# A graph network on one core: edge attributes in loads of 1024 edges, gathers and Relu counted in tiles of edges

## The chip, the cores and the metric

The kernel runs on one core of one Trainium2 chip. Time is the device time of one execution, in microseconds (us). An engine's name stands for its queue too: PE is TensorE, DVE VectorE, ACT ScalarE, POOL GpSimd, SP SyncE. PE multiplies, DVE and ACT work on elements, POOL here issues the indirect DMAs (gathers and scatters, whose addresses come from an index table), SP the plain ones.

## The reference

Four graph layers on 6250 nodes of 96 features and 206,250 directed edges, sorted by destination. The change touches the first two:

```python
h = jnp.maximum(_layernorm(x, axis=-1), 0.0)
# L0
m = h[src] + edge_attr_96                  # [206250, 96]
aggr = jax.ops.segment_sum(m, dst, num_segments=N_NODES)
x = x + (1.0 + eps[0]) * h + relu(aggr @ W1 + b1) @ W2 + b2
# L1
h = jnp.maximum(_layernorm(x, axis=-1), 0.0)
msg = jax.nn.relu(h[src] + edge_attr_32 @ We + be)
aggr = jax.ops.segment_sum(msg, dst, num_segments=N_NODES)
...
```

Behind them come a network of three convolution layers over the same edges and three attention layers with four heads.

## The kernel before

*Tiles, steps and groups.* Edges are cut into 1612 tiles of 128. Nodes are cut into 49 blocks of 128. Because edges are sorted by destination, a tile adds to one block, now and then to two or more; each pair of a tile and a block is a step, padded to 1664 steps. A step is one matmul: a one-hot matrix HOT (128 edges by 128 nodes of the block), built from `REL`, times the tile's 128 rows, into PSUM (`segment_group`, L854, matmul in L860). Eight steps (U) make a group; 208 groups. DVE adds each result to its block of `ACC`, whose number it reads into registers from the table `EB` (`add_up`, L1412, add in L1418). Which edge a step begins at is another row of `EB`, read by SP (`firsts`).

*HOT.* ACT builds it in `hot_of`, eight `Abs` operations (L647) and one `Relu` (L651) per group.

*L0.* A sum over edges of attributes, by `tile_sums` (PE), `load_tiles` (SP, L418) and `sum_stage` (DVE). `load_tiles` issues one DMA of 128 edges (48 KB, L427) per step into four slots of `G`, eight per group, behind the group that used the slot. The sum over neighbours `h[src]` goes another way: POOL scatters edges into a table of counts in DRAM (L582, 1625 indirect DMAs, in the same time as L0's first part), and the stage L0sum (the chase; PE in L885) multiplies strips of that table with the node features, split in bf16 parts by DVE (L1583 to L1585). Then come the layer's small matmuls (L0mlp), the normalisation and the store of the feature table in DRAM.

*L1.* Per group SP loads eight windows of 32 attributes (`load_attrs`, L402), PE transposes them (L966), ACT copies them back (`lift_attrs`, L670), PE multiplies them by We (L971), POOL gathers the rows `h[src]` of eight steps from the feature table (`sums_of`, L527, by `row_of`, L525), DVE adds the products to the gathered rows (`add_product`, L1604), ACT applies the Relu (L675), and PE and DVE sum as in L0. POOL takes the indices from `NOW`, into which DVE copies 16 at a time (L1432) behind the sums of two groups; this copy also tells POOL that the slots are free. All of it is counted in steps: a tile with two blocks is loaded, gathered and rectified twice.

The order on each engine is the order in which its function issues, with loops over four groups (`ROUNDS` = 52).

Of the kernel before, what the change touches and what calls it, by code (L numbers as in the profile page):

```python
# [5 lines left out]
def gnn_kernel(nc, x, src, dst, edge_attr_32, edge_attr_96, L0_W1, L0_b1, L0_W2, L0_b2, L0_eps,  # L6
# [17 lines left out]
    ds = bass.ds  # L24

    P = 128
    N, D = x.shape
# [28 lines left out]
    KC = -(-STEPS // P)  # L56
    WIDE = Q * P
# [16 lines left out]
    assert STRIPS % CHASE_RING == 0 and EP % ROWS_TOGETHER == 0 and 26 - LO_BITS + TALLY_BITS <= 24 and EF < 1 << TALLY_BITS  # L74
    assert SORTED < LOCAL and (PADS + 1) * P * LOCAL < 1 << 26 and SORTED <= 1 << 11

    ctx = ExitStack()
    with ctx:
# [16 lines left out]
        rel_rows = dram("rel_rows", [STEPS, P], bf16)  # L95

# [12 lines left out]
        HOT = sb("HOT", [P, 8, U, P])  # L109
        G = sb("G", [P, 8, U, WT])  # L110
        EA = sb("EA", [P, 2, U * D])
        NOW = sb("NOW", [P, 2, BT], i32)
# [29 lines left out]
        G_flat = G[:, :, :, :].rearrange("p s k d -> p (s k d)")  # L142
        HOT_flat = HOT[:, :, :, :].rearrange("p s k n -> p (s k n)")
# [38 lines left out]
        apart = [HOT[:, 2, :, :], H_flat[:, 0:U * P].rearrange("p (k n) -> p k n", k=U)]  # L182
        row_now = H_flat[:, U * P + TILES:U * P + TILES + 4 * U * P // 2].bitcast(bf16).rearrange("p (b a) -> p b a", b=4)
        assert U * P + TILES + 4 * U * P // 2 <= 3 * STEPS
        REL_neg = [HOT_flat[:, 3 * U * P:3 * U * P + TILES], H_flat[:, U * P:U * P + TILES]]
# [26 lines left out]
        def row(n):  # L212
# [12 lines left out]
        parts_ready = sem("parts_ready")  # L225
        iota_done, consts_done = sem("iota_done"), sem("consts_done")
# [25 lines left out]
        NAMES += [f"strip_in{n}" for n in range(RING)] + [f"tile_in{n}" for n in range(UN)]  # L252
# [8 lines left out]
        gather = {"idx_ready": GROUPS // 2}  # L261
        segment = {"apart_made": GROUPS, "hot_built": GROUPS, "seg_done": GROUPS, "acc_step": TILES}
        PARTED = PARTS + 1
        tiles = {f"tile_in{n}": ROUNDS * U * 16 for n in range(UN)}
# [7 lines left out]
        attrs = {"attr_in0": ITERS * U * 16, "attr_in1": ITERS * U * 16, "rows_ready": GROUPS}  # L272
        dense = {n: NG for n in ("prepared", "staged", "flipped", "lifted", "made", "taken")}
        MOVES = {
            "sum_attr": segment | tiles,
            "sum_relu": gather | segment | attrs | {"ea_flipped": GROUPS, "ea_lifted": GROUPS,
                                                    "ea_product": 2 * GROUPS, "summed": 2 * GROUPS},
# [38 lines left out]
        GATHERED = {name: [sem(f"gathered{slot}_{name}") for slot in range(UN if kind != "attend" else 8)]  # L316
# [14 lines left out]
        def firsts(k, n, engine):  # L331
            return nc.values_load_multi_w_load_instructions(
                EB[32:33, ds(k, n)], engines=(engine,), min_val=0, max_val=E - P,
                skip_runtime_bounds_check_because="the plan clips them")[1]
# [1611 lines left out]
```

## Time and profile before

| | us |
|---|---|
| median of 3 runs | 16749.57 (16744.98 to 16754.85) |
| profiled execution | 16653.95, its span 16652.1 |

| busy, share of the span | |
|---|---|
| PE | 6317.3 us (38%) |
| DVE | 5208.7 us (31%) |
| ACT | 4100.0 us (25%) |
| POOL | 8151.6 us (49%) |

No engine is busy for more than half the span: the kernel is a line of stages, each with its own limit, so shares of the whole say little. The slices of the page show the stages:

```profile
## 2 busy tenths in 40 slices
PE   0100005784444434799433333333333333333333
DVE  6200003422222222322433333343333334333334
POOL 2777771003555555100355555545555554555554
PEclk7555555586566666699655555555555555555555
GB/s 210 11 11 9 9 9 63 81 202 34 39 39 38 39 38 39 95 223 222 82 50 50 52 51 51 51 46 51 50 51 51 51 48 49 51 50 52 52 51 46
```

A slice is 416 us. Slices 2 to 6 are the scatter, in which PE and DVE do next to nothing; slices 7 and 8 are the rest of L0, slice 9 the chase, slices 10 to 16 L1, where POOL is at 5 tenths and PE at 4. From slice 20 on it is attention. In rows of matmuls below, one matmul of float32 counts as two records and two weight loads, so a group of eight steps is 16 records. "Remote" as the end of an idle time means that it was ended by an event that the profile can't put to an instruction close by. "Issue" means that the engine waited for nothing that the profile shows.

### The profile page before, as it was taken

Reading aid. Unit: us, or ns where it says so; the run is one execution under the profiler, and the core shown is the slowest. Engines: PE = TensorE matmul, PEld = TensorE weight load, DVE = VectorE, ACT = ScalarE, POOL = GpSimd, SP = SyncE. Lnnn points to the kernel's source line nnn. Section 1 sums busy time; section 2 is a strip of 40 time slices with the busy share of each in tenths; the row PEclk is TensorE's granted clock in tenths of the full one; section 3 lists DMA queues with packets and bytes.
Section 4 is the critical chain, followed back from the end, with each engine's and each line's share of the span. In section 5 each row is a group of like instructions: output and inputs, shape, how many; then the busy total and the mean of one; then the engine's idle time right before and its main releaser. Section 6 shows DMA issues by size and latency. Waiting matters only on the chain. (4 is left out here: it accounts for less than half of the span.)

```text
span 16652.1 us, 181011 instructions
## 1 busy us (share of the span) xinstructions
PE 6317.3 (38%) x36108; PEld 5357.2 (32%) x36109; DVE 5208.7 (31%) x16216; ACT 4100.0 (25%) x10462; POOL 8151.6 (49%) x8448
## 2 busy tenths in 40 slices
PE   0100005784444434799433333333333333333333
PEld 0000005762332322577432332323223233322332
DVE  6200003422222222322433333343333334333334
ACT  0000005702333333100222222222222222222222
POOL 2777771003555555100355555545555554555554
PEclk7555555586566666699655555555555555555555
DMA  6000002361221112377222222212222222222221
GB/s 210 11 11 9 9 9 63 81 202 34 39 39 38 39 38 39 95 223 222 82 50 50 52 51 51 51 46 51 50 51 51 51 48 49 51 50 52 52 51 46
DMA packets 1157570, 1039.16 MB, mean 62 GB/s; under 512 B 707670, under 2 KB 822582, under 8 KB 1157072
## 3 DMA queue, kind: packets, MB, share of 16 engines
q1 hardware_dynamic: 809536, 614.67, 13.3%
q0 software_dynamic: 265824, 340.03, 10.2%
q10 hardware_dynamic: 81744, 80.28, 1.5%
q14 instruction: 422, 3.46, 0.1%
q8 instruction: 44, 0.72, 0.0%
HBM read 940.04 MB, written 95.72 MB: 62 GB/s over the span
## 5 line engine op out<-in xcount | busy, mean ns | idle before, releaser
L525 POOL DMA_INDIRECT sb_G<-attention_table,sb_NOW x4992 | 4747.6, 951 | 3530.2 <-issue 1460.3
L860 PE MATMUL sums<-sb_G,sb_HOT 128*128 128x100 f32 (+2 forms) x16640 | 3443.1, 394 | 2724.0 <-ACT sb_HOT L651 1248.0
L860 PEld LDWEIGHTS sums<-sb_G,sb_HOT 128*128 128x128 f32 x16640 | 3285.0, 303 | 3012.0 <-issue 2756.1
L525 POOL DMA_INDIRECT sb_G<-feature_table,sb_NOW x1664 | 1573.9, 946 | 1330.8 <-DVE sb_NOW L1432 817.6
L1878 DVE TENSOR_TENSOR sb_ACC<-sb_ACC,sums 128x100 f32 x4992 | 1280.3, 256 | 2825.4 <-issue 1239.5
L582 POOL DMA_INDIRECT edge_counts<-sb_G x1625 | 1734.0, 1067 | 805.8 <-issue 535.3
L1418 DVE TENSOR_TENSOR sb_ACC<-sb_ACC,sums 128x97 f32 (+1 forms) x3328 | 849.9, 255 | 3956.5 <-remote 2447.7
L647 ACT ACTIVATE sb_H<-sb_iota_row,sb_H 128x128 f32<-128x128 f32 x4992 | 1528.7, 389 | 134.3 <-issue 45.5
L647 ACT ACTIVATE sb_HOT<-sb_iota_row,sb_HOT 128x128 f32<-128x128 f32 x3328 | 1015.4, 389 | 2008.8 <-remote 1381.1
L706 ACT ACTIVATE psC<-sb_SB 128x128 f32<-128x128 f32 x156 | 43.8, 281 | 5839.2 <-DVE sb_SB L1831 4863.5
L1037 PE MATMUL psD<-sb_lone,sb_HOT 1*128 1x4 f32 x312 | 90.7, 359 | 2213.3 <-DVE sb_lone L1838 1713.5
L1037 PEld LDWEIGHTS psD<-sb_lone,sb_HOT 1*128 1x128 f32 x312 | 77.2, 305 | 2228.0 <-DVE sb_lone L1838 1649.4
L971 PE MATMUL psB<-sb_WE,sb_EA 128*128 128x384 f32 x416 | 305.6, 833 | 1265.9 <-ACT sb_EA L670 1194.3
L1033 PE MATMUL psD<-sb_LW,sb_ones 128*128 128x128 f32 x312 | 124.1, 501 | 1726.8 <-DVE sb_LW L1796 1112.5
L564 POOL COPY sb_HOT<-sb_H 128x384 f32 (+1 forms) x104 | 54.3, 525 | 1456.4 <-DVE sb_H L1649 1072.3
L651 ACT ACTIVATE sb_HOT<-sb_H 128x1024 f32<-128x1024 f32 x624 | 659.8, 1057 | 66.8 <-remote 47.2
L1033 PEld LDWEIGHTS psD<-sb_LW,sb_ones 128*128 128x128 f32 x312 | 78.2, 311 | 1774.4 <-DVE sb_LW L1796 1143.9
L564 POOL COPY sb_HOT<-sb_ACC 128x384 f32 (+1 forms) x26 | 13.1, 508 | 1283.5 <-DVE sb_plan L1465 1202.4
L1750 DVE TENSOR_SCALAR sb_EA<-sb_H,sb_iota_col 128x1024 bf16<-128x1024 bf16 x624 | 293.8, 492 | 1087.9 <-remote 566.7
L1855 DVE TENSOR_TENSOR sb_G<-sb_G,psC 128x768 f32<-128x768 f32 x624 | 565.4, 948 | 3.6 <-issue 0.6
L670 ACT ACTIVATE sb_EA<-psA 128x256 f32<-128x256 f32 x208 | 79.9, 384 | 1921.3 <-remote 1490.4
L971 PEld LDWEIGHTS psB<-sb_WE,sb_EA 128*128 128x128 f32 x416 | 94.1, 282 | 1334.1 <-issue 1318.7
(435 smaller groups left out, 8993.4 us busy)
## 6 DMA issues: line engine op xcount, KB each, us to landing
sb_G<-edge_counts SPq DMA_DIRECT2D x1152, 256.0 KB, 3.3
sb_H<-rel_rows SPq DMA_DIRECT2D x624, 256.0 KB
sb_G<-in_edge_attr_dram SPq DMA_DIRECT2D x1664, 48.0 KB
sb_G<-attention_table,sb_NOW POOLq DMA_INDIRECT x4992
edge_counts<-sb_LW ACTq DMA_DIRECT2D x12, 6272.0 KB, 42.5
sb_EA<-in_edge_attr_dram SPq DMA_DIRECT2D x1664, 16.0 KB
sb_G<-feature_table,sb_NOW POOLq DMA_INDIRECT x1664
edge_counts<-sb_G POOLq DMA_INDIRECT x1625
```

Of the source, the lines that this page charges most:

```text
L525: pool.indirect_dma_start(to, None, rows, bass.IndirectOffsetOnAxis(ap=index, axis=0)).then_inc(landed, 16)
L582: pool.indirect_dma_start(every_count, bass.IndirectOffsetOnAxis(ap=slot_of[:, f:f + 1], axis=0), tally[:, f:f + 1], None).then_inc(scatte ...
L647: last = nc.scalar.activation(apart[place][:, c, :], iota_row[:, :], ACT.Abs, bias=REL_neg[place][:, ds(k + c, 1)])
L651: nc.scalar.activation(HOT[:, to, :, :], apart[place], ACT.Relu, bias=1.0, scale=-1.0)\
L860: last = nc.tensor.matmul(bank[:, k // 4, k % 4 * width:(k % 4 + 1) * width], HOT[:, hot, k, :], G[:, slot, k, 0:width], start=True, stop= ...
L971: nc.tensor.matmul((psB, psC)[q][:, 0:4 * D], EA[:, half, U * DE + q * P:U * DE + (q + 1) * P], WE[:, :, :].rearrange("p a b -> p (a b)"), ...
L1033: last = nc.tensor.matmul(psD[:, P:2 * P], ones[:, :], LW[:, 2, 0:P], start=True, stop=True)
L1037: last = nc.tensor.matmul(psD[:, 3 * P:3 * P + HEADS], HOT[0:1, BG * half, 0, :], lone[0:1, 4:8], start=True, stop=True)
L1418: v.tensor_tensor(to, to, sums[n % 2][:, k // 4, k % 4 * width:(k % 4 + 1) * width], ALU.add)\
L1750: v.tensor_scalar(ST[n % 2], row_now[:, n % 4, :].rearrange("p (k e) -> p k e", k=U), iota_col[:, 0:1], None, ALU.is_equal).then_inc(SEM[" ...
L1855: v.tensor_tensor(rows, rows, w.unsqueeze(3).broadcast_to([P, U, HEADS, C]), ALU.mult)\
L1878: v.tensor_tensor(to, to, sums[group % 2][:, k % U // 4, k % 4 * WT:(k % 4 + 1) * WT], ALU.add)\
```

## The change

*L0.* `load_tiles` loads 1024 edges (eight whole tiles, 384 KB) with one DMA into `ring0`, a ring of ten loads (80 tile places), 202 loads in place of 1664. Steps read the place of their tile in the ring from a new row of `EB`: PE loads eight places into registers per group (`places`, `sum_steps`), and each matmul addresses the ring by a register. A tile with two blocks is loaded once. Load g waits until g − 3 groups are summed, and group g waits for load g.

*L1.* One DMA per 1024 edges of attributes, 202 groups of products; POOL gathers tile by tile (1612 gathers) into `ring1` of twelve groups, waits ahead of gathers g until g − 5 groups are summed (`seg_done`), and for indices once per 48; add_product and Relu run once per tile, 202 groups; PE's sums address `ring1` by registers too. HOT's differences are built in another buffer (place=1).

*Indices by tile.* Ahead of the chase ACT loads the sources tile by tile, DVE casts them, PE transposes them in 13 pieces, DVE copies them out, and ACT stores them (`src_cols`) and loads them again as `cols_now` beside the chase. Two rows of places are computed on DVE in the setup.

```diff
+    LOADS = -(-ET // U)
+    LAST_LOAD = ET - (LOADS - 1) * U
+    LAG = -(-(NB - 1) // U)
+    RING0, RING1, SIX = 10, 12, 6
...
+        def places(ring, k, n, engine):
+
+            row, top = (32, RING0 * U - 1) if ring is ring0 else (0, RING1 * U - 1)
             return nc.values_load_multi_w_load_instructions(
-                EB[32:33, ds(k, n)], engines=(engine,), min_val=0, max_val=E - P,
+                EB[row:row + 1, ds(k, n)], engines=(engine,), min_val=0, max_val=top,
...
+            def load_attrs(t, attr):
+
+                to = [EA[:, half, 0:U * DE].rearrange("p (k d) -> p k d", k=U) for half in range(2)]
+
+                def load(g, half):
+                    sp.dma_start(to[half], tiles_of(attr, U * g, U)).then_inc(SEM[f"attr_in{half}"], 16)
...
             def load_tiles(t, attr):
 
-                with sp.Fori(0, ROUNDS) as it:
-                    for half in range(2):
-                        e = firsts(UN * U * it + 2 * U * half, 2 * U, SP)
-                        for j in range(2 * half, 2 * half + 2):
-
-                            sp.wait_ge(SEM["seg_done"], UN * it + (freed(t, UN) + j + 1))
-                            for n in range(U):
-                                sp.dma_start(G[:, j, n, 0:D], attr[ds(e[j % 2 * U + n], P), :])\
-                                  .then_inc(SEM[f"tile_in{j}"], 16)
+                def emptied(g):
+
+                    sp.wait_ge(SEM["seg_done"], g + (t.base["seg_done"] + LAG + 1 - RING0))
+
+                def load(g, slot):
+                    emptied(g)
+                    sp.dma_start(ring0[:, U * slot:U * (slot + 1), 0:D], tiles_of(attr, U * g, U)).then_inc(attr_in[slot], 16)
...
             sp.wait_ge(rel_rows_made, 1)
             sp.dma_start(rel_rows.rearrange("(c p) e -> p c e", p=P), rel_row).then_inc(rel_rows_stored, 16)
+            sp.wait_ge(rel_rows_stored, 16)
...
             def sums_of(t):
 
-                with pool.Fori(0, ROUNDS) as it:
-                    for pair in range(UN // 2):
-
-
-                        pool.wait_ge(SEM["idx_ready"], UN // 2 * it + (t.base["idx_ready"] + pair + 1))
-                        pool.sem_inc(idx_seen, 1)
-                        for n in range(2 * U):
-                            slot = 2 * pair + n // U
-                            row_of(G[:, slot, n % U, 0:D], NOW[:, pair, n:n + 1], table, t.gathered[slot])
+                def rows(g, six, slot, tiles):
+
+                    pool.wait_ge(SEM["seg_done"], g + (t.base["seg_done"] + LAG + 1 - RING1))
+                    if slot % SIX == 0:
+
+                        pool.wait_ge(SEM["idx_ready"], six + (t.base["idx_ready"] + 1))
+                    pool.sem_inc(idx_seen, 1)
+                    for n in range(tiles):
+                        at = slot % SIX * U + n
+                        row_of(ring1[:, U * slot + n, :], NOW[:, slot // SIX, at:at + 1], table, t.gathered[slot % SIX])
...
+            act.wait_ge(rows_in, 5 * 16)
+            act.wait_ge(parts_ready, 1)
+            full = ET // P * P
+            act.dma_start(src_tiles[:, 0:full].rearrange("p (c e) -> p c e", e=P),
+                          src_rows[0:full, :].rearrange("(c t) e -> t c e", t=P)).then_inc(tiles_loaded, 16)
...
+            act.wait_ge(cols_made, 1)
+            act.dma_start(src_cols, src_turned[:, 0:SIXES * SIX * U]).then_inc(cols_stored, 16)
...
+            act.dma_start(cols_now, src_cols).then_inc(cols_in, 16)
...
-                nc.scalar.activation(G[:, half, :, 0:D], G[:, half, :, 0:D], ACT.Relu).then_inc(SEM["rows_ready"], 1)
+                rows = ring1[:, ds(U * slot, U), :]
+                nc.scalar.activation(rows, rows, ACT.Relu).then_inc(SEM["rows_ready"], 1)
...
+            def sum_steps(t, g, half, ring, width):
+
+                place = places(ring, U * g, U, PE)
+                pe.wait_ge(SEM["acc_step"], U * g + (t.base["acc_step"] - U))
+                pe.wait_ge(SEM["hot_built"], g + (t.base["hot_built"] + 1))
+                for k in range(U):
+                    last = nc.tensor.matmul(sums[half][:, k // 4, k % 4 * width:(k % 4 + 1) * width], HOT[:, half, k, :],
+                                            ring[:, ds(place[k], 1), 0:width].squeeze(1), start=True, stop=True)
+                last.then_inc(SEM["seg_done"], 1)
...
-            pe.wait_ge(parts_ready, 1)
+            pe.wait_ge(tiles_cast, 1)
+            for c in range(KC):
+                last = nc.tensor.transpose(sums[c // 8][:, c // 4 % 2, c % 4 * P:(c % 4 + 1) * P],
+                                           src_turning[:, c * P:(c + 1) * P], ident[:, :])
+            last.then_inc(tiles_turned, 1)
+            pe.wait_ge(cols_made, 1)
             chase_stage(Stage("L0sum"))
...
+            def turn(g, half, nth, products=True, rows=True):
+
+                if products:
+                    attr_product(half + 1, 16 * nth + t.base[f"attr_in{1 - half}"], g + 2, g + 1)
+                if rows:
+                    pe.wait_ge(SEM["rows_ready"], g + (t.base["rows_ready"] + 1))
+                sum_steps(t, g, half, ring1, D)
...
+            dve.wait_ge(tiles_loaded, 32)
+            v.tensor_copy(src_turning, src_tiles).then_inc(tiles_cast, 1)
+            dve.wait_ge(tiles_turned, 1)
...
+            last.then_inc(cols_made, 1)
             dve.wait_ge(zeroed, 16 * NG)
             chase_sums(Stage("L0sum"))
```

On SP, in L0's loop, stood this before; `sb_G` is the ring of four slots, L332 the register load of the edges at which steps begin:

```order
L332 TENSOR_LOAD sb_EB
L425 ISA
L427 ISA [waits seg_done]
L427 DMA sb_G<-in_edge_attr_dram 128x96
L427 ISA
L427 DMA sb_G<-in_edge_attr_dram 128x96
```

and now this, for two groups (`sb_HG` holds `ring0`):

```order
L465 ISA
L462 ISA [waits seg_done]
L462 DMA sb_HG<-in_edge_attr_dram 128x8x96
L458 REGISTER_ALU
L462 ISA [waits seg_done]
L462 DMA sb_HG<-in_edge_attr_dram 128x8x96
L458 REGISTER_ALU
```

The register loads are gone from SP, and eight pairs of a register step and a DMA have become one.

On PE, one group of L0 was this before:

```order
L868 ISA [waits hot_built]
L858 ISA [waits tile_in0]
L860 MATMUL sums<-sb_G,sb_HOT 128x97 [waits acc_step]
L860 MATMUL sums<-sb_G,sb_HOT 128x97 x7
L867 REGISTER_ALU
```

and is now this (the two last rows stand eight times in all):

```order
L354 ISA [waits attr_in_ring0]
L354 TENSOR_LOAD sb_EB
L934 REGISTER_ALU
L935 REGISTER_ALU [waits acc_step]
L937 ISA [waits hot_built]
L937 MATMUL sums<-sb_HG 128x97
L937 ISA
L937 MATMUL sums<-sb_HG 128x97
```

The load of places has come to PE, ahead of the waits for DVE's adds and for HOT, and a register operation has come between any two matmuls. In L1 the same rows stand behind the wait for `rows_ready`.

On POOL, L1's gathers stood like this before, 16 behind one wait for indices:

```order
L529 ISA
L525 DMA sb_G<-feature_table,sb_NOW 128x96 [waits idx_ready]
L525 DMA sb_G<-feature_table,sb_NOW 128x96 x15
L533 REGISTER_ALU
L525 DMA sb_G<-feature_table,sb_NOW 128x96 [waits idx_ready]
```

and stand like this now:

```order
L579 ISA [waits seg_done]
L570 DMA sb_HG<-feature_table,sb_NOW 128x96 [waits idx_ready]
L570 DMA sb_HG<-feature_table,sb_NOW 128x96 x7
L576 REGISTER_ALU
L570 DMA sb_HG<-feature_table,sb_NOW 128x96 [waits seg_done]
L570 DMA sb_HG<-feature_table,sb_NOW 128x96 x7
```

A wait for a summed group has come ahead of every eight gathers, and the wait for indices stands at every sixth of them.

## Rows read from the trace of the kernel before

**Rows 1.** Windows: busy us of each engine (records), granted clock, DMA share, GB/s.

```profile
647.00:2560.00 1913.00, 167.60 (x720) 156.94 (x720) 92.83 (x345) 157.45 (x405) 1451.23 (x1383) 0.50 0.06 10
2600.00:3380.00 780.00, 587.82 (x2560) 550.22 (x2560) 331.18 (x1288) 564.17 (x1449) 0.00 (x0) 0.51 0.35 80
...
3440.00:3770.00 330.00, 311.38 (x2558) 238.26 (x2556) 40.24 (x93) 0.28 (x1) 1.02 (x3) 0.99 0.76 237
...
3880.00:6740.00 2860.00, 1225.32 (x4596) 833.25 (x4597) 650.88 (x2187) 939.44 (x2291) 1575.87 (x1668) 0.62 0.20 38
```

**Rows 2.** Timeline of DVE beside the scatter: start us, us, operation, idle before it.

```profile
1556.40 3.06 DVE L1418 TENSOR_TENSOR sb_ACC<-sb_ACC,sums 128x97 f32 x8 [41.89 <-remote]
```

**Rows 3.** SP's line L427, 700 to 2560 us: min/median/max ns; who waited.

```profile
L427 SPq DMA_DIRECT2D sb_G<-in_edge_attr_dram x351: 8/699/1400, 701.1 to 2560.0; - x176
...
  PE sums L860: 199.0, 6
```

**Rows 4.** The same line, 2700 to 3300 us.

```profile
L427 SPq DMA_DIRECT2D sb_G<-in_edge_attr_dram x986: 332/333/333, 2699.8 to 3300.0; - x198
```

**Rows 5.** Timeline of SP beside the scatter.

```profile
1517.60 24.53 SPq L427 DMA_DIRECT2D sb_G<-in_edge_attr_dram  x7
```

**Rows 6.** PE's line L860, 2600 to 3400 us: idle before it, us and times.

```profile
  DVE sb_ACC L1418: 330.8, 244
  DMA sb_G<-in_edge_attr_dram: 88.7, 66
```

**Rows 7.** Timeline of DVE after the scatter.

```profile
2912.49 3.06 DVE L1418 TENSOR_TENSOR sb_ACC<-sb_ACC,sums 128x97 f32 x8 [1.32 <-PE sums L860]
2917.98 3.06 DVE L1418 TENSOR_TENSOR sb_ACC<-sb_ACC,sums 128x97 f32 x8 [2.43 <-PE sums L860]
2921.99 3.06 DVE L1418 TENSOR_TENSOR sb_ACC<-sb_ACC,sums 128x97 f32 x8 [0.95 <-PE sums L860]
```

**Rows 8.** Groups by line, 3880 to 6740 us: busy us, mean ns, idle before.

```profile
L525 POOL DMA_INDIRECT sb_G<-feature_table,sb_NOW x1664 | 1573.9, 946 | 1330.8 <-DVE sb_NOW L1432 817.6 <-issue 513.2
```

**Rows 9.** Timelines of POOL and DVE in L1.

```profile
4915.81 0.95 POOL L525 DMA_INDIRECT sb_G<-feature_table,sb_NOW  x1 [0.30 <-issue]
4923.87 0.95 POOL L525 DMA_INDIRECT sb_G<-feature_table,sb_NOW  x1 [7.11 <-DVE sb_NOW L1432]
...
4919.71 3.03 DVE L1418 TENSOR_TENSOR sb_ACC<-sb_ACC,sums 128x96 f32 x8 [10.23 <-remote]
...
4928.32 3.03 DVE L1418 TENSOR_TENSOR sb_ACC<-sb_ACC,sums 128x96 f32 x8 [4.29 <-PE sums L860]
```

**Rows 10.** Timeline of DVE in the setup.

```profile
480.18 1.03 DVE L1318 CAST sb_H<-sb_H 128x1664 f32<-128x1664 int32 x1 [138.72 <-DMA sb_H<-dst_rows,sb_row_i]
```

**Rows 11.** Line L337, register loads and steps on PE's queue (PEldq), ns.

```profile
L337 PEldq TENSOR_LOAD <-sb_EB x624: 587/591/775, 8095.8 to 16593.6; - x156
L337 PEldq FUSED_REGOPS  x600: 46/46/51, 8198.7 to 16551.5; - x150
```

**Rows 12.** Timeline at the end of L0.

```profile
3389.63 3.06 DVE L1418 TENSOR_TENSOR sb_ACC<-sb_ACC,sums 128x97 f32 x8 [1.18 <-PE sums L860]
...
3430.63 1.62 PE L885 MATMUL sums<-sb_HOT,sb_G 128*128 128x288 bf16 x6 [41.14 <-DVE sb_HOT L1585]
```

**Rows 13.** DMAs by what they move: KB each, median us to landing.

```profile
feature_table<-sb_ACC SPq DMA_DIRECT2D x1, 2496.0 KB, 10.9
```

**Rows 14.** Groups by line, whole span: PE, then DVE.

```profile
L783 PE MATMUL sums<-sb_ident,sb_H 128*128 128x128 f32 x13 | 5.3, 412 | 141.6 <-DVE sb_G L1319 141.6
...
L1329 DVE CAST sb_IDX<-sums 128x512 int32<-128x512 f32 (+1 forms) x4 | 2.4, 592 | 0.1
```

**Rows 15.** Timeline of POOL in attention.

```profile
9020.20 0.95 POOL L525 DMA_INDIRECT sb_G<-attention_table,sb_NOW  x1 [3.79 <-remote]
...
9054.19 0.95 POOL L525 DMA_INDIRECT sb_G<-attention_table,sb_NOW  x1 [13.43 <-PE sums L860]
```

**Rows 16.** Line L525 from 8100 us on: min/median/max ns, first, last start.

```profile
L525 POOL DMA_INDIRECT sb_G<-attention_table,sb_NOW x4992: 942/947/1209, 8106.0 to 16565.8; - x200
```

## What I predicted before the run

> **What bounds the kernel now.** I read the windows by stage first, then for each stage that the change touches its groups by line, its waits, and the timeline of a few groups. The profiled execution took 16653.95 us (span 16652.1).
>
> The windows [rows 1] show the four stretches that the change touches. From 647 to 2560 us POOL is busy for 1451 of 1913 us with the scatter (L582) while PE does 720 matmul records beside it. One group of eight steps is 16 records, so that is 45 of 208 groups. From 2600 to 3380 POOL is silent and PE does 2560 records, 160 groups in 780 us: 4.87 us each. From 3440 to 3770 the chase keeps PE busy for 311 of 330 us. From 3880 to 6740 L1 runs, with POOL the busiest engine at 1576 of 2860 us. What follows 6740 keeps its instructions.
>
> *L0 beside the scatter.* DVE adds up one group in 3.06 us and idles for 41.9 us before it [rows 2]: a group takes 44.9 us here and 4.87 us later, with the same work. The adds are not slower themselves (3.06 us in both, rows 2 and 7). What is slow are SP's queue steps: the issue of a DMA has a median of 699 ns here and 333 ns after the scatter [rows 3, 4]. Seven issues take 24.53 us [rows 5], 4.0 us from one to the next with three instructions each (register operation, move, issue), so about 1.3 us per instruction, near twice 0.7. I read this as one path, taken up while POOL issues DMAs back to back, that lets one instruction through per 0.7 us and that SP and PE use in turn. The count bears it out: per group SP has 8 times 3 and about 2 more for the register loads, PE 32 records and about 4 register and wait steps, 62 to 64 together; 64 times 0.7 is 44.8 us.
>
> *L0 after the scatter.* PE's sums wait 330.8 us on DVE's adds and 88.7 us on attributes [rows 6]. DVE's groups of 3.06 us start 5.49 and 4.01 us apart [rows 7]. The shorter is what the chain of PE and DVE does when the tile is there; SP's eight issues, with their register loads, make the rest.
>
> *L1.* POOL's 1664 gathers of 946 ns leave it idle for 1330.8 us, 817.6 of them on DVE's copy of indices (L1432) and 513.2 between issues [rows 8]: 1252 ns per gather while it issues. Around 4900 us [rows 9] a burst of 16 ends at 4916.76 and POOL then waits 7.11 us until DVE has copied the next 16 indices: 19.7 and 7.1 us, 27 for two groups, 13.5 to 13.7 each. DVE's adds idle 10.23 us there "until remote", and are released 2.95 us after POOL's last gather: the same slow spell. The next group, out of the spell, is added up 8.61 us later. So L1 is a loop: a burst of gathers, a spell in which the news that a group is summed comes late, and a restart that waits for that news.
>
> **The change part by part.** Durations are of the profiled execution; the median of the runs shown (16749.57) is 96 us longer, and I carry a difference in us over to it unscaled.
>
> *Rows of places.* Twelve more DVE operations of 1664 elements on one row, at 1.03 us or up to twice that: 12 to 25 us. They stand ahead of the 138.72 us in which DVE waits for dst_rows [rows 10]. Cost 0; without this cover up to 25.
>
> *L0 beside the scatter.* SP goes from about 26 instructions per group to 4. PE gains per group a register load, three register and wait steps and a register operation for each matmul: 12 beside 32 records, 44. By the count above 48 times 0.7 is 33.6 us, and I take 34. About 1900 us of scatter then hold 56 groups instead of 45. Bounds: if PE alone sets the pace (44.9 over 36 is 1.25 each), 44 times 1.25 is 54.8 us and some 37 groups; on the other side the case in which the spell goes altogether, a rival below.
>
> *L0 after the scatter.* 152 groups instead of some 162. A load of 1024 edges is one issue, made once the group four before is summed: 13 us ahead, against 10.9 us for a transfer six times its size in rows 13. So SP no longer decides. PE's register load is 591 ns and a register step 46 ns [rows 11]. They stand ahead of the wait for DVE's adds and run while the matmuls of the group before are still queued, so PE needs 3.7 to 4.7 us. I take 4.25 us, between the 4.01 of rows 7 and 4.7; bounds 3.9 and 4.87. 152 times 4.25 is 646 us: L0 ends near 2576 + 646 = 3222 instead of 3392.7, where its last adds end [rows 12], 170 us earlier. With 54.8 and 4.87 it would be 171 groups in 833 us, an end near 3409 and a loss of 17; with 34 and 3.9 the gain is 224. A group in 4.25 us asks for 0.39 MB, 92 GB/s; this stretch moves 80 now and the chase 237 [rows 1], so the transfers are not the bound.
>
> The Trainium skill (DMA: Bandwidth & Descriptors, Rules for kernel authors) says to coalesce many small transfers, since under 64 KB one pays mostly overhead. By it the 48 KB tiles are the fault in both stretches. The trace agrees after the scatter, where SP's steps fill the gap; beside the scatter PE waits 199.0 us of 1913 for attributes [rows 3], so size is not what holds it there. By that rule alone L0 would end with the scatter, which I do not follow.
>
> *In front of the chase.* PE starts the chase at 3430.63, behind DVE's last cast [rows 12]. Between them come now a load of the sources as tiles (806 KB; 2496 KB take 10.9 us, a third of it 3.6 [rows 13]), a cast like the one of 1.03 us in rows 10, 13 transposes of 5.3 us and four copies of 2.4 us in all [rows 14]. That is 12 to 20 us, and with the handovers between four queues I take 20; bounds 10 and 40. The store and the load of 0.84 MB run beside the chase, 7 us at 237 GB/s if nothing hides them; PE is the bound there, so 0.
>
> *L1.* 202 groups instead of 208, 1612 gathers instead of 1664. POOL asks that the group six before is summed and issues eight gathers, instead of 16 per copy of indices. The ring holds twelve groups. A burst of eight takes 8 times 1.252 less the last pause, 9.7 us. What follows it is the question. Attention runs POOL so already, eight gathers per group summed [rows 15]: a gap of 3.79 us ahead of 9020.20, next to none within the 16 gathers that follow, then 13.43 us. Its 4992 gathers lie between 8106.0 and 16565.8 [rows 16], 13.6 us per group with all that lies between its layers, and its groups are more work. I take 3.15 us, near the 2.95 from the last gather to the release in rows 9: 12.9 us per group. 202 times 12.9 is 2606, and the last six groups without gathers and the start some 65: 2671. Now it is 208 times 13.7, 2851. Gain 180. Bounds: POOL without any gap, 10.05 us per group, a gain of 755; a gap of 7.1 us behind every eight (as now behind every sixteen), 16.8 us, a loss of 610. Of the gaps the 3.79 of rows 15 stands in the same setting, so I stay near it.
>
> *Sum.* −170 + 20 − 180 = −330: 16654 becomes 16324, and 16750 becomes 16420.
>
> **The rivals.**
>
> *A. POOL runs through in L1.* For it: a group out of the spell takes 8.61 us, less than POOL's 10.05, and the ring of twelve lets POOL be five groups ahead. Against it: beside the scatter a group in a lasting spell takes 44.9 us, so PE falls behind until the ring is full and POOL must wait; attention with its ring of eight does that. At 10.05 to 11.5 us (10.8): 202 × 10.8 + 65 = 2247, a gain of 604, with the other terms 754: 15996.
>
> *B. SP's own eight DMAs per group make the spells.* For it: SP's steps are what the profile shows slow in L0. Then L0 ends inside the scatter, the chase begins near 2600 instead of 3430 (830 less), and L1 is POOL's 10.05 (755 less): 15165. Against it: POOL in attention waits 13.43 us for PE's sums [rows 15] with a single load per group on SP. Beside it stands a sentence of the Trainium skill (DMA: Bandwidth & Descriptors, SWDGE vs HWDGE vs iDMA): DMAs issued by SP never touch the ring state that GpSimd writes. Taken widely it would leave SP's issues alone while POOL issues; rows 3 and 4 show 699 ns against 333, and the measurement decides.
>
> *C. Slower: L1's restarts feed the spell.* POOL restarts at each sum, so a new spell begins about as PE starts the next one, and PE is later by its register load and steps, which stand behind the wait for the rows (591 + 12 × 46, 1.1 us). If this pushes the news of each group behind the end of the burst, POOL waits 7.1 us or more behind each eight. It decides from a gap of 4.1 us on (2851 less 65 is 2786, over 202 is 13.8, less 9.7). At 7.1 us L1 takes 3459, a loss of 608, and with L0's 150 less the total is 17208. For it: the 13.43 in rows 15. Against it: the 3.79 there and the 16 gathers almost without a gap, and that five groups lie between POOL and PE instead of two to four.
>
> *D. Nothing to measure.* L0 at 54.8 us per group beside the scatter and L1 at 13.8.
>
> **How the numbers follow.** The forecast, 16420, has 0.60, with a range of its own of 16250 to 16620. A has 0.16, B 0.04, C 0.14, D 0.06. About 0.2% (33 us) is what a measurement of this kernel can tell from no change. Faster by more: the forecast, A, B and a little of D, 0.81; within it 0.06; slower 0.13. The range from 15880 to 16860 leaves out B, the low edge of A and most of C.
>
> **What would show it.** Right: DVE's adds beside the scatter 32 to 36 us apart; after it PE's groups 4.1 to 4.4 us apart; PE's first chase matmul 15 to 30 us behind the last cast; POOL in bursts of eight with gaps of 2.5 to 4 us in L1. Wrong: adds beside the scatter still 45 us apart or more (PE's records alone set the spell) or 4 to 9 us (B), POOL without gaps (A), gaps over 5 us behind each burst (C), or PE waiting for attributes behind the big load.

## The result, and the profile after

The changed kernel took 16241.22 us (median of 4 runs, 16235.82 to 16251.36), the kernel before 16750.93 in the same comparison: ratio 0.9697, 95% interval 0.968 to 0.9714. That is 510 us less; 330 were forecast. In the profiled executions the difference is 418 us (16652.1 and 16233.8 us of span), since the one of before was 97 us under its median. A second pair on one chip (c1 and c2 below) gave 16602.74 and 16113.32 us, ratio 0.9703; in its two traces the difference is 473 us.

Windows of the changed kernel, columns as in rows 1:

```profile
647.00:2560.00 1913.00, 162.72 (x704) 152.61 (x704) 97.24 (x344) 155.28 (x401) 1451.39 (x1373) 0.50 0.06 10
...
3000.00:3100.00 100.00, 90.67 (x392) 84.98 (x391) 50.08 (x195) 85.34 (x222) 0.00 (x0) 0.50 0.38 97
```

Beside the scatter nothing has moved: 704 records, 44 groups, against 45 [rows 1]. After it 392 records in 100 us are 24.5 groups, 4.08 us each against 4.87; over all 164 groups of this stretch it is 4.11 us against 4.82. The timelines of PE and DVE beside the scatter, then of SP's line L462 (min/median/max ns):

```profile
1028.65 3.72 PE L937 MATMUL sums<-sb_HG 128*128 x16 [41.36 <-issue]
...
1024.91 3.06 DVE L1512 TENSOR_TENSOR sb_ACC<-sb_ACC,sums 128x97 f32 x8 [42.02 <-remote]
1069.99 3.06 DVE L1512 TENSOR_TENSOR sb_ACC<-sb_ACC,sums 128x97 f32 x8 [42.02 <-remote]
```

```profile
L462 SPq DMA_DIRECT2D sb_HG<-in_edge_attr_dram x42: 367/373/377, 709.3 to 2558.7; - x42
```

PE's matmuls end at 1032.37 and DVE adds their results from 1069.99 on, 37.6 us later; for most of that time only POOL works. A group takes 45.1 us, as before (44.9, rows 2). SP now issues once per group, at the moment when the news comes, and in 373 ns.

At the end of L0 and in front of the chase:

```profile
3292.06 3.06 DVE L1512 TENSOR_TENSOR sb_ACC<-sb_ACC,sums 128x97 f32 x8 [0.98 <-DVE sb_ACC L1512]
...
3338.14 1.03 DVE L1653 CAST sb_H<-sb_H 128x1664 f32<-128x1664 int32 x1 [5.34 <-DMA sb_H<-src_rows]
3339.28 2.63 PEld L1036 LDWEIGHTS sums<-sb_ident,sb_H 128*128 128x128 f32 x13 [48.62 <-issue]
3339.32 3.01 PE L1036 MATMUL sums<-sb_ident,sb_H 128*128 128x128 f32 x13 [48.41 <-DVE sb_H L1653]
3342.36 2.08 DVE L1657 CAST sb_H<-sums 128x512 int32<-128x512 f32 x4 [3.19 <-PE sums L1036]
...
3344.78 7.93 PE L966 MATMUL sums<-sb_HG 128*128 128x288 bf16 x48 [2.46 <-DVE sb_H L1657]
```

L0's last adds end at 3295.1 instead of 3392.7 [rows 12], 98 us earlier, although the scatter's last DMA starts at 2593.1 and not at 2576.0. Between the end of the last cast (3332.8) and the first matmul of the chase lie 12.0 us instead of 0.4.

L1 by lines (columns as in rows 8), and POOL and DVE in a piece of it:

```profile
L570 POOL DMA_INDIRECT sb_HG<-feature_table,sb_NOW x1612 | 1524.6, 946 | 966.8 <-issue 463.4 <-remote 405.9 <-DVE sb_NOW L1685 65.4
```

```profile
4807.85 0.95 POOL L570 DMA_INDIRECT sb_HG<-feature_table,sb_NOW  x1 [4.42 <-remote]
...
4832.85 0.95 POOL L570 DMA_INDIRECT sb_HG<-feature_table,sb_NOW  x1 [4.13 <-remote]
...
4856.77 0.95 POOL L570 DMA_INDIRECT sb_HG<-feature_table,sb_NOW  x1 [4.21 <-remote]
...
4807.11 3.03 DVE L1512 TENSOR_TENSOR sb_ACC<-sb_ACC,sums 128x96 f32 x8 [0.50 <-remote]
...
4832.11 3.03 DVE L1512 TENSOR_TENSOR sb_ACC<-sb_ACC,sums 128x96 f32 x8 [3.98 <-remote]
```

Bursts of sixteen gathers now start 24 to 25 us apart here, instead of 27 [rows 9]. Counted over all of L1, the trace has 100 gaps of more than 1.9 us between gathers, 84 of the 99 distances between them are sixteen gathers, and the median gap is 3.5 us; before it was 100 gaps, 97 distances of sixteen, and 7.3 us. So the bursts have kept their length, although POOL now asks ahead of every eight, and the gap has become shorter. The first gather starts at 3799.2 and the last at 6224.3: 2425 us, 12.0 per group of 202, against 2838 (3881.2 to 6719.6). POOL starts 0.74 us after DVE has the news (4807.85 and 4807.11), where it used to start 4.16 us after (4923.87 and 4919.71, rows 9): DVE's adds and copy no longer stand in between.

The difference of 413 us splits by rows 8 and the row above: 49 us busy and 50 us between issues, both with 52 gathers fewer, and 314 us of waiting (817.6 less 65.4 at the start, against 405.9 and 32.2 on sums). Part of it comes back at the end. Behind the start of the last gather DVE adds up twelve more groups, six of which have no gathers of their own:

```profile
6229.43 3.03 DVE L1512 TENSOR_TENSOR sb_ACC<-sb_ACC,sums 128x96 f32 x8 [5.40 <-PE sums L937]
...
6280.36 3.03 DVE L1512 TENSOR_TENSOR sb_ACC<-sb_ACC,sums 128x96 f32 x8 [0.79 <-DVE sb_ACC L1512]
6284.18 3.03 DVE L1512 TENSOR_TENSOR sb_ACC<-sb_ACC,sums 128x96 f32 x8 [0.79 <-PE sums L937]
```

The first six are 8.9 to 9.8 us apart and the last ones 3.82, up to 6302.6: 78 us from the last gather on, where it was 11.

### The profile page after: what moved, and what is told of

It is laid out like the page before. It is cut to its first block, busy times and chain, and to the rows that moved or that the text cites. A ratio compares the mean times of both kernels' runs of the same rounds, so it can differ in the third digit from the quotient of the medians.

```text
span 16233.8 us, 175253 instructions
## 1 busy us (share of the span) xinstructions
PE 6413.5 (40%) x36085; PEld 5433.4 (33%) x36086; DVE 5208.3 (32%) x16151; ACT 4094.3 (25%) x10450; POOL 8110.2 (50%) x8396
## 4 chain that ended last, share of the span: by engine, by line
another core or an unknown queue 26%; issue 25%; DVE 17%; PE 16%; DVEq 11%; ACT 4%; DMA 1%; ACTq 1%; SPq 0%; POOL 0%; POOLq 0%; PEldq 0%
PE sums L927 5%; DVE sb_ACC L1973 4%; PE sums L995 3%; DVEq L1973 3%; DVE sb_ACC L1512 3%; ACT sb_H L699 2%; DVEq L1971 2%; DVEq L362 2%; DVE sb_EA L1845 1%; ACT sb_HG L739 1%; PE sums L966 1%; DVE sb_HG L1950 1%; DVEq L1830 1%; PE sums L937 1%
## 5 line engine op out<-in xcount | busy, mean ns | idle before, releaser
L570 POOL DMA_INDIRECT sb_HG<-attention_table,sb_NOW x4992 | 4741.1, 950 | 3566.9 <-issue 1454.7
L937 PE MATMUL sums<-sb_HG 128*128 x6656 | 1446.8, 405 | 2418.1 <-issue 2243.7
L937 PEld LDWEIGHTS sums<-sb_HG 128*128 128x128 f32 x6656 | 1351.0, 310 | 2691.1 <-issue 2691.1
L927 PE MATMUL sums<-sb_HG 128*128 128x100 f32 x9984 | 2065.4, 398 | 364.5 <-DVE sb_HG L1950 345.7
L634 POOL DMA_INDIRECT edge_counts<-sb_HG x1625 | 1748.2, 1076 | 808.7 <-issue 539.2
L927 PEld LDWEIGHTS sums<-sb_HG 128*128 128x128 f32 x9984 | 1998.3, 308 | 393.7 <-issue 378.1
L699 ACT ACTIVATE sb_H<-sb_iota_row,sb_H 128x128 f32<-128x128 f32 x6656 | 2037.1, 388 | 151.7 <-issue 54.3
L570 POOL DMA_INDIRECT sb_HG<-feature_table,sb_NOW x1612 | 1524.6, 946 | 966.8 <-issue 463.4
L699 ACT ACTIVATE sb_EA<-sb_iota_row,sb_HG 128x128 f32<-128x128 f32 x1664 | 508.6, 387 | 1905.7 <-remote 1764.4
L703 ACT ACTIVATE sb_HG<-sb_H 128x1024 f32<-128x1024 f32 x832 | 879.2, 1057 | 75.0 <-issue 25.1
L1950 DVE TENSOR_TENSOR sb_HG<-sb_HG,psC 128x768 f32<-128x768 f32 x624 | 565.1, 947 | 0.0
```

Source lines behind the costliest of these rows:

```text
L570: pool.indirect_dma_start(to, None, rows, bass.IndirectOffsetOnAxis(ap=index, axis=0)).then_inc(landed, 16)
L634: pool.indirect_dma_start(every_count, bass.IndirectOffsetOnAxis(ap=slot_of[:, f:f + 1], axis=0), tally[:, f:f + 1], None).then_inc(scatte ...
L699: last = nc.scalar.activation(apart[place][:, c, :], iota_row[:, :], ACT.Abs, bias=REL_neg[place][:, ds(k + c, 1)])
L703: nc.scalar.activation(HOT[:, to, :, :], apart[place], ACT.Relu, bias=1.0, scale=-1.0)\
L927: last = nc.tensor.matmul(bank[:, k // 4, k % 4 * width:(k % 4 + 1) * width], HOT[:, hot, k, :], G[:, slot, k, 0:width], start=True, stop= ...
L937: last = nc.tensor.matmul(sums[half][:, k // 4, k % 4 * width:(k % 4 + 1) * width], HOT[:, half, k, :], ring[:, ds(place[k], 1), 0:width]. ...
```

## The experiments

The runs came to several chips, and these fell into two kinds, which nobody chose. On one kind (the comparison above, and c1 to c4 on chip 11) the kernel before takes 16587 to 16755 us; on the other (e on chip 10, d and f on chip 14) its medians are 12618 to 12637. Each experiment is read within its kind. No chip was seen in both kinds, but chip 14 alone was used twice, so it is not shown that the kind belongs to the chip and not to the time of the run.

### e1: eight DMAs per group again

```diff
-                    sp.dma_start(ring0[:, U * slot:U * (slot + 1), 0:D], tiles_of(attr, U * g, U)).then_inc(attr_in[slot], 16)
+                    for n in range(U):
+                        sp.dma_start(ring0[:, U * slot + n, 0:D], attr[ds(P * U * g + P * n, P), :]).then_inc(attr_in[slot], 16)
```

> The changed kernel, but L0 loads each 1024 edges in eight DMAs of 128 edges again (same ring, same waits). Compared with the changed kernel. Theory of the prediction (SP and PE share one path, 0.7 us per instruction): SP's instructions per group rise from 4 to about 20, a group beside the scatter takes 64 x 0.7 = 45 us and more, clearly longer than in the changed kernel if that count were what matters there. Rival (SP's instructions cost nothing beside the scatter, since the wait there is for PE's news alone): adds stay 45.1 us apart there, and only the stretch after the scatter changes, from 4.3 to about 4.6 to 4.9 us per group for some 163 groups: L0 ends 50 to 95 us later, the total is longer by as much.

(PE's waits count the eight DMAs of a load accordingly.) 12587.92 us against 12617.65 of before, ratio 0.9977 (0.9967 to 0.9987). There was no late news to test, and L0 is over at 1515 us, inside the scatter, so nothing that it costs can show in the total. It says nothing on either theory of the lateness. Its trace does say what the transfers themselves cost where the news is on time: groups are 4.33 us apart against 4.12 in e3 on the same chip, which loads 1024 edges at once, and L0 ends 48 us later (1515 against 1467). The expectation had 4.6 to 4.9.

### e2 and f1: every matmul of L0's sums twice

```diff
-                for k in range(U):
+                for k in [k for k in range(U) for _ in range(2 if ring is ring0 else 1)]:
```

> The changed kernel, but every matmul of L0's sums is issued twice (64 instead of 32 records and weight loads per group; the second overwrites the first). Rival A (beside the scatter PE's news comes only after each of its matmul and weight records has passed, about 1.3 us each): adds are 82 to 87 us apart beside the scatter, some 24 groups done by its end. Rival B (the news is late by a fixed 37 us, whatever PE did): 49 us apart. The theory of the prediction (0.7 us per instruction, 76 of PE and 4 of SP): 56 us. After the scatter PE alone sets 7.5 to 8 us per group in all cases, so the total grows by about 600 (B) to 750 us (A).

> As e2: every matmul of L0's sums issued twice. On a chip on which PE's news is late: 82 to 87 us between adds beside the scatter if the news waits for each of PE's matmul and weight records (A), 49 us if it is late by a fixed time (B), 56 us by the prediction's count of instructions. On a chip without late news nothing is learned.

12596.12 and 12599.29 us (one run each; before 12617.65 and 12636.71). L0 lies beside the scatter here, so the total could not show it; but the groups did not become slower either. They are 4.11 us apart, as in e3 (4.12), where PE alone was expected to need 7.5 to 8. Windows of e2, then of e3:

```profile
700.00:1400.00 700.00, 647.94 (x5445) 620.77 (x5446) 349.86 (x1361) 596.23 (x1533) 530.75 (x556) 1.00 0.41 96
...
700.00:1400.00 700.00, 619.24 (x2724) 579.44 (x2723) 349.82 (x1362) 595.41 (x1531) 531.07 (x555) 0.52 0.40 96
```

With 32 matmul records per group the granted clock was 1.00 (2.4 GHz), with 16 it was 0.52, almost all of it the lower level of 1.2 GHz. So the 32 records of a group took 3.81 us, where 16 take 3.72: twice the work in the same time. What the lateness depends on could not be learned, since both runs came to chips without it.

### e3, d2 and f2: L1 asks once per two groups; e4: asks three groups nearer

```diff
-                    pool.wait_ge(SEM["seg_done"], g + (t.base["seg_done"] + LAG + 1 - RING1))
+                    if slot % 2 == 0:
+                        pool.wait_ge(SEM["seg_done"], g + (t.base["seg_done"] + LAG + 2 - RING1))
```

and in e4 `LAG + 4` in the first of these lines.

> The changed kernel, but in L1 POOL asks for summed groups only ahead of every second group and for both at once, so that it issues 16 gathers in a burst as before the change; ring, tiles and everything else stay. If L1's gain comes from bursts of eight (finer asking), L1 goes back to about 13.5 us per group, from 12.0: 300 us longer. If it comes from being released by the sum itself rather than by DVE's copy, or from the deeper ring, L1 stays near 12.0 to 12.5 and the total within 100 us.

> The changed kernel, but in L1 POOL waits until g - 2 groups are summed before it gathers for group g, instead of g - 5: bursts of eight stay, the depth that the ring allows is not used. If depth is what gains, POOL waits longer for each group and L1 goes to 14 us per group and more (400 us longer). If POOL is always at the limit of the wait anyway (it restarts at the news of each group whatever the distance), only the start differs, and the total stays within 50 us.

> As e3: in L1 POOL asks once per two groups and for both at once, 16 gathers in a burst. On a chip on which PE's news is late: if bursts of eight are what gained in L1, 13.5 us per group and 300 us more than the changed kernel's 2387 us of gathers; if the release by the sum itself and the depth of five groups are, near 12 us and no more than 100 us. On a chip without late news: no difference, 2011 us.

> As d2: in L1 POOL issues 16 gathers per asking. On a chip on which PE's news is late: L1's gathers last 2387 us in the changed kernel (11.9 per group); some 2700 if bursts of eight are what gained, below 2490 if the release by the sum and the depth of five groups are.

e3 12587.59 (0.9976, 0.9967 to 0.9986), e4 12588.14 (0.9975), d2 12599.68 (0.9981, 0.9972 to 0.9991), f2 12614.94 us against 12636.71 (one run each). All came to the second kind of chip. POOL's line there, in e3 (from 2600 to 4700 us, with its idle time):

```profile
L570 POOL DMA_INDIRECT sb_HG<-feature_table,sb_NOW x1612: 940/944/1000, 2611.8 to 4622.9; - x180
...
  issue: 491.0, 1611
  DVE sb_NOW L1686: 65.4, 1
```

POOL never waits for a sum: 2011 us for 1612 gathers, 9.96 per group. So how and how far ahead it asks makes no difference there, and which of burst, depth and direct release gained L1's time on the first kind of chip was not measured by a run. The trace of the changed kernel narrows it: its bursts were still sixteen gathers long, so bursts of eight are not what gained.

The same kernel beside the scatter, timelines of DVE and POOL:

```profile
1002.77 3.06 DVE L1513 TENSOR_TENSOR sb_ACC<-sb_ACC,sums 128x97 f32 x8 [0.98 <-DVE sb_ACC L1513]
1007.10 3.06 DVE L1513 TENSOR_TENSOR sb_ACC<-sb_ACC,sums 128x97 f32 x8 [1.27 <-issue]
...
1002.80 0.96 POOL L635 DMA_INDIRECT edge_counts<-sb_HG  x1 [0.30 <-issue]
1004.07 0.95 POOL L635 DMA_INDIRECT edge_counts<-sb_HG  x1 [0.30 <-issue]
```

The groups are 4.04 and 4.33 us apart and not 45. Adds last as long as on the other chips (3.06 us), and so does the median scatter (0.96 us). POOL's stream is not quite the same, though. On the first kind its scatters become longer around each release of the news:

```profile
1070.13 1.12 POOL L634 DMA_INDIRECT edge_counts<-sb_HG  x1 [0.30 <-issue]
1072.14 1.91 POOL L634 DMA_INDIRECT edge_counts<-sb_HG  x1 [0.89 <-issue]
```

From the first scatter to the last it takes 2319 us in the changed kernel there (274.0 to 2593.1) and 2158 in e3 (274.5 to 2432.4). So most of the difference between the kinds is the news that comes late or on time, and 140 to 160 us of it are POOL's own slower stream.

### c1 and c2: both kernels, unchanged

> The kernel before, unchanged, for a trace of it on the chip of the experiments, where its time was 12618 us and not 16750. If the late news from PE (adds beside the scatter 44.9 us apart, L1 at 13.7 us per group) is what is missing there, L0 is over before the scatter ends, L1's gathers go without gaps (1664 x 1.25 = 2080 us), and attention's 4992 gathers too (2090 us per layer instead of 2740). If instead the whole chip is faster, single gathers and adds are shorter as well (946 and 257 ns here).

> The changed kernel, unchanged, on the chip of the experiments. Where PE's news is not late, L0 costs nothing beside the scatter, and what is left of the change is 52 gathers fewer (65 us) less the work in front of the chase (12 us): some 50 us, 0.4%, faster than before, 12565 to 12590. Where the news is late, 16240 against 16750 again.

c1 16591.81 us, c2 16113.32 (5 runs) against 16602.74, 0.9703 (0.969 to 0.9717). This chip is of the first kind. c1 repeats the trace before: 720 records from 647 to 2560 us, L1's gathers over 2838 us, attention's over 2721 to 2738 us a layer. On the other kind (e3) attention takes 2089 to 2095 us a layer. The second case of each expectation, a chip without late news, could not be seen for these two kernels. The variants e1, e3, e4 and d2 come near it: their traces show L0 inside the scatter or POOL never waiting in L1, and their gain over before is 0.19 to 0.25%, 20 to 30 us. That the unaltered change gains as much there is an inference and was not run.

### c3 and c4: the scatter waits for L0

```diff
+    START_GATE, GATE, GATE_GROUPS = 240, 6, 1
...
+                        issued += 1
+                        if issued >= START_GATE and (issued - START_GATE) % GATE == 0 and asked + GATE_GROUPS <= GROUPS:
+                            asked += GATE_GROUPS
+                            pool.wait_ge(SEM["seg_done"], Stage("L0").base["seg_done"] + asked)
```

In c4 `GATE_GROUPS` is 2.

> The changed kernel, but POOL's scatter pauses: after every six of its DMAs it waits for one more group of L0 to be summed. Where PE's news is late while POOL issues without a pause: a group every 11 to 12 us beside the scatter instead of 45, all 208 groups by about 3000 us, L0 ends some 250 us earlier. Where the news is not late: the scatter is held up by nothing (a group takes less than six DMAs' 7.6 us), no difference.

> The same, but two more groups asked for after every six DMAs. Late news: the first group comes 3 us after POOL stops and the second 4 to 9 us later, so a turn takes 16 us for two groups: L0 done by about 2350 us and the scatter by 3100 (or earlier if both come together). Not late: two groups at about 4.3 us each need 8.6 us against the six DMAs' 7.6, so the scatter is held up by 1 us per turn, some 100 us in all.

c3 took 15455.53 us and c4 15517.74 (one run each) on the chip where the changed kernel takes 16113.32. For c3 that is 658 us less, 4.1%, and 6.9% less than before. The window of c3 beside the scatter, and POOL, DVE and PE in it:

```profile
647.00:2560.00 1913.00, 791.02 (x3441) 733.22 (x3441) 480.50 (x1687) 728.76 (x1874) 1281.32 (x1317) 0.51 0.19 44
```

```profile
1011.94 0.96 POOL L636 DMA_INDIRECT edge_counts<-sb_HG  x1 [0.30 <-issue]
1015.43 0.96 POOL L636 DMA_INDIRECT edge_counts<-sb_HG  x1 [2.53 <-remote]
...
1032.66 0.96 POOL L636 DMA_INDIRECT edge_counts<-sb_HG  x1 [2.39 <-remote]
...
1015.29 3.06 DVE L1518 TENSOR_TENSOR sb_ACC<-sb_ACC,sums 128x97 f32 x8 [9.78 <-remote]
...
1001.68 3.72 PE L943 MATMUL sums<-sb_HG 128*128 x16 [7.38 <-DVE sb_ACC L1518]
1006.20 3.72 PE L943 MATMUL sums<-sb_HG 128*128 x16 [0.80 <-issue]
```

PE's matmuls of two groups end at 1005.4 and 1009.9. POOL stops at 1012.9, and at 1015.29, 2.4 us after, DVE, PE and POOL all go on. That repeats every 17.2 us (12 DMAs, two groups). Adding POOL's pauses is the only edit, and with them the news comes 9.9 us after the first group's matmuls (1005.4 to 1015.29) instead of 37.6: the pause of POOL is what lets it through. L0 is done at 2467 us and the scatter at 2662 instead of 2580, 82 us later; L1's first gather comes at 3109.9 instead of 3783.2. I had expected a group every 11 to 12 us, L0 done by about 3000 and 250 us gained. It was 8.7 us per group, since each pause lets two groups' news through, and the gain was more than twice as large.

c4 asks for two groups per six DMAs. L0 is then done at 1706 us, a group in 5.0 us, because the pauses, 2 to 4 us after each six DMAs, come before much lateness has gathered: of two groups the first has its matmuls done at 1013.8 and is added up from 1016.86, 3 us later and 1.4 after POOL stopped. But the scatter ends at 2759, 180 us later than in c2, and the chase waits for the scatter. c3 pays less for what it hides. My expectation for c4 had L0 ending at 2350 and the scatter at 3100, both too late, since I had put 16 us on a turn that takes 10.1.

### d1: the better of the two, timed

> The changed kernel with POOL's scatter waiting for one more summed group of L0 after every six DMAs, timed in rounds. Where PE's news is late (before near 16600 to 16750 us): 15450 to 15600, ratio 0.930 to 0.935 to the kernel before and some 4% under the changed kernel. Where the news is not late (before near 12618): the waits hold nothing up, 12560 to 12600 as the changed kernel.

12602.07 us against 12619.44, ratio 0.9985 (0.9976 to 0.9994), on a chip of the second kind. I had expected 12560 to 12600. There the waits gain nothing: d2, without them on the same chip, takes 12599.68 (0.9981), and the intervals overlap. On the first kind c3 rests on its one run.

## Why the prediction came out as it did

*L0 beside the scatter: wrong.* I predicted 34 us per group from a count of instructions (64 before, 48 after, at 0.7 us). Measured: 45.1. The count fitted 44.8 by chance. SP went from 26 to 4 instructions and PE from 36 to 44, 48 instead of 62 to 64 in all, and the lateness stayed where it was. So the step that failed is the shared path with a price per instruction. The forecast's own sign against it, adds still 45 us apart, is what came. Before, PE's matmuls were these:

```profile
1515.18 3.73 PE L860 MATMUL sums<-sb_G,sb_HOT 128*128 128x97 f32 x16 [40.98 <-ACT sb_HOT L651]
```

Their end, 1518.91, lies 37.5 us ahead of the adds at 1556.40 [rows 2]; after the change it is 37.6. SP's slow steps were not the cause. They still occur with one DMA per group: the register step behind SP's DMA takes 2.1 us beside the scatter and 37 ns after it, and a group still takes 45.1 us. That step's line in the changed kernel, 700 to 2560 us and 2700 to 3200 us (min/median/max ns):

```profile
L458 SPq ALU_OP  x38: 1410/2097/2098, 710.5 to 2559.9; - x38
L458 SPq ALU_OP  x109: 32/37/37, 2703.3 to 3195.3; - x109
```

c3 and c4 show the cause as far as the runs go: POOL's DMAs without a pause, and on some chips alone. L0's groups before and after share PE's 32 matmul and weight records, so they can't tell a delay per record from a fixed one. A place in the setup, beside the same scatter, has another count. There PE does 26 matmuls with their weight loads in a row, 52 records, and DVE waits for them: PE's last matmul and DVE's start in the kernel before, then in e3:

```profile
487.52 0.27 PE L784 MATMUL psD<-sb_ident,sb_G 128*128 128x128 f32 x1
526.59 1.89 DVE L1321 TENSOR_TENSOR sb_HOT<-sb_iota_row,sb_lane_tiles 128x1664 f32<-128x1664 f32 x1 [44.32 <-remote]
...
492.73 0.42 PE L852 MATMUL psD<-sb_ident,sb_HG 128*128 128x128 f32 x1
493.19 1.89 DVE L1415 TENSOR_TENSOR sb_HG<-sb_iota_row,sb_lane_tiles 128x1664 f32<-128x1664 f32 x1 [5.90 <-PE psD L852]
```

The news is 38.8 us late in the kernel before (40.2 and 41.6 in the first comparison's changed kernel and in c2) and on time in e3. A delay per record would make it 61 us (37.5 over 32, times 52; an estimate). So the traces speak for a nearly fixed delay; no run tested it on L0's sums. My theory had a forecast for a kernel that I already had (the change itself), and there it failed; the tests with doubled matmuls stayed open.

*L0 after the scatter: right in its pace.* 4.25 us predicted, 4.11 measured over the stretch. It took 98 us off, not 170, for two reasons. There were 164 groups left and not 152. And the fast stretch began at 2621.7 and not at 2576, where I had put it: the scatter ended 17 us later, and two more groups were added late, at 2603.1 and 2621.7. With 152 groups left it would have been 147 us (an estimate from the same rows).

*In front of the chase: right in kind, 12 us instead of 20.* The load took 5.3 us, the transposes 3.0 instead of 5.3. The clock is not the reason (0.50 granted here, 0.54 there). I had read rows 14 wrongly: the 5.3 us are the sum of 13 matmuls of 412 ns that overlap with 13 others, and in the setup all 26 together take 5.5 us.

*L1: right in kind, wrong in form and size.* Bursts separated by pauses, as forecast, and no free run. But the bursts are of sixteen gathers and not of eight: I put 3.15 us behind every eight, and a pair of groups has 4.3 us in all (438 us over 101 pairs), not 6.3, nearly all of it in one gap. At every other asking the news is nearly there; that the next sums are already under way by then is my reading and was not tested. So 12.0 us per group instead of 12.9, 180 us more. What became shorter against before is that one gap, by 3.8 us at the median (7.3 to 3.5). About 3.4 us of it fits the shorter way from the news to POOL (4.16 to 0.74 us in the pieces shown); what the deeper ring gave was not separated. Against that the tail was larger than my 65 us for start and tail together: 78 us from the last gather on. From the first gather to the last adds L1 gained 346 us (2850 to 2503), where 180 were forecast.

*The sum.* −98 + 12 − 346 is −432, against −330. The other 14 of 418 lie in stages that are not touched, with 20 less between L1 and attention and 30 more in attention. One term was too large by 72 us and one too small by 166, so that the sum came out even as near as it did is partly luck. The rest of the 510 us, 92, lies in the kernel before's profiled execution, which was 97 us under its median; its cause is open. c1 and c2 repeat the split: 108 us less up to the end of L0, 383 in L1.

*The rivals.* A (no gaps in L1) is what the second kind of chip does, 9.96 us per group, and not the first. B (SP's DMAs make the spells) is refuted by the change itself: one DMA per group, the same 45.1 us. C (restarts feed the spell): gaps of 4.1 to 4.4 us are there in the piece shown, just where C would begin to cost, but behind sixteen gathers and not behind eight. D (54.8 us per group beside the scatter, L1 at 13.8) did not come in either part. The Trainium skill (DMA: Bandwidth & Descriptors, SWDGE vs HWDGE vs iDMA) says that DMAs issued by SP never touch the ring state that GpSimd writes. The runs are not against that sentence: SP's DMA issue takes 373 ns beside the scatter and 373 ns after it. In the kernel before, where eight of them followed each other, the issues took 699 ns [rows 3], but so did the moves and register steps between them (700 ns). So the DMA as such is not what is slow there.

The rule of the Trainium skill to coalesce small transfers (DMA: Bandwidth & Descriptors, Rules for kernel authors) did not help beside the scatter: eight times larger transfers brought nothing there (44.9 and 45.1 us per group). After it the change brought 0.7 to 0.8 us per group. By e1 only 0.2 of that is the number of transfers, if the second kind of chip tells for the first; the rest must lie in the other parts of the change, such as the register loads that left SP and the tiles that are now loaded once, which were not separated.

## What to carry to other kernels

When one engine issues DMAs back to back and others idle "until remote", look for the time from the end of the producer's work to the consumer's start. Here the wait ended 2 to 3 us after the stream's pause, and pauses were worth more (658 us) than all the fewer instructions and transfers (98 us in L0). Put them where something is due (a wait for the consumer's own progress), and count what they take from the stream. Do not fit a delay by a count of instructions without a second kernel, or a second place in the trace, in which the count differs. Look at the granted clock before you expect twice the matmuls to take twice the time (e2). And time a kernel on more than one chip before calling such a delay a property of the kernel.

## What the runs showed of the hardware that I had not expected

The same kernel before took 16587 to 16755 us on some chips and 12618 to 12637 (medians) on others, about 25% less, with equal median durations of single operations (adds 3.06 us per eight, scatters 0.96 us; the mean scatter is 1067 ns before and 1004 ns in e3). Most of the difference is the lateness of PE's news while POOL streams: 37.5 us beside the scatter, or none. The change gains 3.0% on the first kind, and its variants gain 0.19 to 0.25% on the second; the pauses of c3 gain 4.1% more on the first (one run) and nothing on the second (d1). Why the chips differ is open. Twice the matmuls of L0 took no longer, since the granted clock was 1.00 with them and 0.52 without (e2, e3).
